# Attention of an AdaLN block: the maxima of two PSUM banks in one VectorE instruction, and the softmax sums dealt out anew between VectorE and GpSimd

## What is computed

```python
pattern = jnp.einsum('bhid,bhjd->bhij', k, q) * scale      # 2048 keys i by 2048 queries j, for 2 x 16 heads
prob = jax.nn.softmax(pattern, axis=-2)                     # over the keys
out = jnp.einsum('bhis,bhid->bhsd', prob, v)
x = x + ga * (concat(out) @ Wo + bo)
```

## Time and profile before

| | us |
|---|---|
| median of 3 runs (4717.35 to 4722.87) | 4717.73 |
| the profiled execution, its own time | 4722.76 |
| its span, first to last instruction | 4721.0 |
| mean granted TensorE clock | 0.972 of full |

### The profile page before, as it was taken

One profiled execution on the slowest core, in us unless ns is written; L12 is line 12 of the kernel. 1 busy time (PEld: TensorE's weight loads), 2 busy tenths in 40 slices (PEclk: granted clock), 3 DMA queues, 4 the chain that ended last, 5 costly groups with the idle time before them and its releaser, 6 DMA issues.

```text
span 4721.0 us, 67306 instructions
## 1 busy us (share of the span) xinstructions
PE 4368.3 (93%) x25496; PEld 2574.1 (55%) x25496; DVE 3253.8 (69%) x4370; ACT 2169.1 (46%) x3523; POOL 2907.6 (62%) x1269
## 2 busy tenths in 40 slices
PE   7999999999999999999999999759998896989898
PEld 5545454454454454554545544337676675767575
DVE  6777877878777877778777787455654545665455
ACT  5444444444444444444444444326565434556442
POOL 2867767667667677677676676526665334666332
PEclk8999999999999999999999999879999998999899
DMA  2000000000000000000000000100000000000001
GB/s 78 6 11 14 7 11 7 14 11 5 15 11 5 11 15 6 11 13 8 11 6 15 11 5 7 40 18 1 1 1 5 33 1 19 1 1 1 1 1 36
DMA packets 81402, 55.74 MB, mean 12 GB/s; under 512 B 48532, under 2 KB 71016, under 8 KB 81128
## 3 DMA queue, kind: packets, MB, share of 16 engines
q1 hardware_dynamic: 81128, 51.92, 4.1%
HBM read 30.66 MB, written 4.19 MB: 7 GB/s over the span
## 4 chain that ended last, share of the span: by engine, by line
POOL 53%; issue 21%; PE 12%; DVE 8%; ACT 4%; POOLq 1%; DMA 0%; DVEq 0%; SPq 0%; ACTq 0%
POOL accp L770 41%; POOL lp L792 4%; PE psum L1665 4%; POOL accp L766 3%; PE psum L1794 2%; POOL rnorm L782 2%; POOL qk_u L787 2%; PE psum L1807 2%; DVE ssq L1262 1%; ACT lp L974 1%; PE psum L1711 1%; ACT qk_sq L958 1%; DVE qk_w L1274 1%; POOL ug_l L820 1%; DVE lneg L1288 1%
## 5 line engine op out<-in xcount | busy, mean ns | idle before, releaser
L770 POOL TENSOR_TENSOR accp<-accp,prob 128x1024 f32<-128x1024 f32 x704 | 1766.9, 2510 | 492.5 <-ACT prob L928 414.0
L928 ACT ACTIVATE prob<-psum 128x1024 f32<-128x1024 f32 x1024 | 1020.0, 1024 | 1461.4 <-PE psum L1518 1383.6
L1159 DVE TENSOR_REDUCE mx<-psum 128x1 f32<-128x512 f32 x1984 | 1276.2, 684 | 347.2 <-PE psum L1485 298.0
L1530 PE MATMUL psum<-prob,vv 128*64 128x512 f32 x4096 | 993.2, 606 | 0.0
L1485 PE MATMUL psum<-kh,qh 64*128 64x512 f32 x2048 | 493.6, 471 | 56.1 <-DVE mx L1159 48.7
L1530 PEld LDWEIGHTS psum<-prob,vv 128*64 128x64 f32 x4096 | 248.7, 136 | 490.3 <-issue 427.3
L1485 PEld LDWEIGHTS psum<-kh,qh 64*128 64x128 f32 x2048 | 205.3, 185 | 522.6 <-DVE mx L1159 442.0
L792 POOL TENSOR_TENSOR lp<-lp,lrcp 128x1024 f32<-128x1024 f32 x128 | 297.9, 2327 | 238.0 <-DVE lrcp L1294 238.0
L1518 PE MATMUL psum<-nm,one 64*128 64x512 f32 x2048 | 428.7, 408 | 13.9 <-ACT prob L928 6.5
L1518 PE MATMUL psum<-qh,kh 64*128 64x512 f32 x2048 | 412.2, 391 | 0.0
L1518 PE MATMUL psum<-qh,kl 64*128 64x512 f32 x2048 | 412.1, 391 | 0.0
(11 more groups left out here) (197 smaller groups left out, 6942.3 us busy)
## 6 DMA issues: line engine op xcount, KB each, us to landing
kl<-kl SPq DMA_DIRECT2D x64, 256.0 KB, 3.8
wqk<-L_attn_Wq SPq DMA_DIRECT2D x64, 64.0 KB, 2.0
rot_l<-const_rot SPq DMA_DIRECT2D x2, 2048.0 KB, 9.3
out<-lpT SPq DMA_DIRECT2D x32, 128.0 KB, 1.7
wqkv_l<-L_ffn_wqkv SPq DMA_DIRECT2D x4, 768.0 KB, 10.7
w_l<-L_ffn_w SPq DMA_DIRECT2D x4, 618.0 KB
wqk<-L_attn_Wk SPq DMA_DIRECT2D x32, 64.0 KB, 2.0
wv_p<-L_attn_Wv SPq DMA_DIRECT2D x16, 128.0 KB, 2.2
```

The source lines that it names most:

```text
L770: pool.tensor_tensor(acc_p[cp][:], first[:], prob[kt % PRING][:], ALU.add).then_inc(pool_sum, 1)
L928: act.activation(prob[t % PRING][:], psum[:, S_BANK + 2 * (t % 2):S_BANK + 2 * (t % 2) + 2, :].rearrange("p a b -> p (a b)"), ACT.Exp, sca ...
L1159: dve.tensor_reduce(mx4[:, e, qt, c:c + 1], ps, AX_X, ALU.max).then_inc(ring_free, 1)
L1530: mm = pe.matmul(psum[j * DH:(j + 1) * DH, O_BANK, :], vv[:, kt, s * DH:(s + 1) * DH], prob[t % PRING][:, j * T:(j + 1) * T], start=(kt == ...
```

## The change

The first two tiles of a VectorE sum are added in one instruction, straight into `acc_d`, in place of a copy and an addition, so a half costs VectorE two instructions and not three (`DVE_OPS`). VectorE's tiles become 8, 10, 12 in half 0 and 1, 3, 10 in half 1. The first addition stands at the values of the second tile. Its first tile stays unread until then, and the exponential that reuses its slot waits for that (`dve_used`). The weights of groups 11 and 12 become 2 and 3. A couple whose two places are neighbouring banks is reduced by one instruction, which frees both places when it ends.

```diff
--- before.py
+++ after.py
@@ -36,13 +36,13 @@
 CP = CHUNKS // 2
 STEPS = CP * KT
 PRING = 4
-SUM_DVE = (3, 7, 11)
-SUM_POOL = tuple(k for k in range(KT) if k not in SUM_DVE)
+SUM_DVE = ((8, 10, 12), (1, 3, 10))
+SUM_POOL = tuple(tuple(k for k in range(KT) if k not in tiles) for tiles in SUM_DVE)
 
 JOIN = -1
-POOL_SEQ = SUM_POOL[1:-1] + (JOIN,) + SUM_POOL[-1:]
-POOL_OPS = len(POOL_SEQ)
-DVE_OPS = len(SUM_DVE)
+POOL_SEQ = tuple(tiles[1:-1] + (JOIN,) + tiles[-1:] for tiles in SUM_POOL)
+POOL_OPS = len(POOL_SEQ[0])
+DVE_OPS = len(SUM_DVE[0]) - 1
 QK_ITEMS, V_ITEMS = CHUNKS, 4
 V_TILES = KT // V_ITEMS
 WO_ITEMS = CHUNKS * HALVES
@@ -307,7 +307,7 @@
 
             weight = [4] * (GROUPS - 1) + [0]
             weight[0] = 1
-            weight[SUM0_GROUP + 1:SUM0_GROUP + 3] = [0, 2]
+            weight[SUM0_GROUP + 1:SUM0_GROUP + 3] = [2, 3]
             for g in outs:
                 weight[g] = 3
             return [-(-COUPLES * sum(weight[:g + 1]) // sum(weight)) for g in range(GROUPS)]
@@ -406,9 +406,13 @@
 
         OFF_S, OFF_POOL, OFF_DVE, OFF_RING = STEPS, CP * POOL_OPS, CP * DVE_OPS, RING_PAIR
 
-        def pool_used(kt):
-
-            return 1 if kt == SUM_POOL[0] else POOL_SEQ.index(kt) + 1
+        def pool_used(cp, kt):
+
+            return 1 if kt == SUM_POOL[cp][0] else POOL_SEQ[cp].index(kt) + 1
+
+        def dve_used(cp, kt):
+
+            return max(SUM_DVE[cp].index(kt), 1)
 
         def phase_end(eng, phase):
 
@@ -758,7 +762,7 @@
             def head_sums(G):
 
                 for cp in range(CP):
-                    for i, kt in enumerate(POOL_SEQ):
+                    for i, kt in enumerate(POOL_SEQ[cp]):
                         n = G * (CP * POOL_OPS) + OFF_POOL + cp * POOL_OPS + i
                         pool.wait_ge(pool_sum, n)
                         if kt == JOIN:
@@ -766,7 +770,7 @@
                             pool.tensor_tensor(acc_p[cp][:], acc_p[cp][:], acc_d[cp][:], ALU.add).then_inc(pool_sum, 1)
                             continue
                         pool.wait_ge(exp_done, G * STEPS + cp * KT + kt + 1)
-                        first = acc_p[cp] if i else prob[SUM_POOL[0] % PRING]
+                        first = acc_p[cp] if i else prob[SUM_POOL[cp][0] % PRING]
                         pool.tensor_tensor(acc_p[cp][:], first[:], prob[kt % PRING][:], ALU.add).then_inc(pool_sum, 1)
 
             with pool.Fori(0, ALL_PAIRS) as p:
@@ -921,10 +925,10 @@
 
                     act.wait_ge(pv_done, G * STEPS + OFF_S + t - PRING + 1)
                     cp, kt = divmod(t - PRING, KT)
-                    if kt in SUM_DVE:
-                        act.wait_ge(dve_sum, G * (CP * DVE_OPS) + OFF_DVE + cp * DVE_OPS + SUM_DVE.index(kt) + 1)
+                    if kt in SUM_DVE[cp % CP]:
+                        act.wait_ge(dve_sum, G * (CP * DVE_OPS) + OFF_DVE + cp * DVE_OPS + dve_used(cp % CP, kt))
                     else:
-                        act.wait_ge(pool_sum, G * (CP * POOL_OPS) + OFF_POOL + cp * POOL_OPS + pool_used(kt))
+                        act.wait_ge(pool_sum, G * (CP * POOL_OPS) + OFF_POOL + cp * POOL_OPS + pool_used(cp % CP, kt))
                     act.activation(prob[t % PRING][:], psum[:, S_BANK + 2 * (t % 2):S_BANK + 2 * (t % 2) + 2, :].rearrange("p a b -> p (a b)"),
                                    ACT.Exp, scale=float(ATT_SCALE)).then_inc(exp_done, 1)
                     if t == KT + 1:
@@ -1154,6 +1158,11 @@
 
             def max_couple(rb, r, k):
                 qt, c = divmod(k, CHUNKS)
+                if (r + 1) % RING:
+                    ring_wait(rb, r + 1)
+                    bank = M_BANK + r % RING
+                    dve.tensor_reduce(mx4[:, :, qt, c], psum[:, bank:bank + 2, :], AX_X, ALU.max).then_inc(ring_free, 2)
+                    return
                 for e in range(2):
                     ps = ring_wait(rb, r + e)
                     dve.tensor_reduce(mx4[:, e, qt, c:c + 1], ps, AX_X, ALU.max).then_inc(ring_free, 1)
@@ -1175,13 +1184,13 @@
                 op.then_inc(ring_free, count)
 
             def add_sum(G, cp, j):
-                kt = SUM_DVE[j]
-                dve.wait_ge(exp_done, G * STEPS + cp * KT + kt + 1)
-                if j:
-                    dve.wait_ge(dve_sum, G * (CP * DVE_OPS) + OFF_DVE + cp * DVE_OPS + j)
-                    dve.tensor_tensor(acc_d[cp][:], acc_d[cp][:], prob[kt % PRING][:], ALU.add).then_inc(dve_sum, 1)
-                else:
-                    dve.tensor_copy(acc_d[cp][:], prob[kt % PRING][:]).then_inc(dve_sum, 1)
+                tiles = SUM_DVE[cp]
+                dve.wait_ge(exp_done, G * STEPS + cp * KT + tiles[j] + 1)
+                left = prob[tiles[0] % PRING]
+                if j > 1:
+                    dve.wait_ge(dve_sum, G * (CP * DVE_OPS) + OFF_DVE + cp * DVE_OPS + j - 1)
+                    left = acc_d[cp]
+                dve.tensor_tensor(acc_d[cp][:], left[:], prob[tiles[j] % PRING][:], ALU.add).then_inc(dve_sum, 1)
 
             def normalise(G, rb, i, hh, cp):
                 ps = ring_wait(rb, i)
@@ -1217,8 +1226,8 @@
                             next_hidden(rb, r, j, places(kind, j, hh))
                         elif kind == "values":
                             cp, kt = divmod(j, KT)
-                            if kt in SUM_DVE:
-                                add_sum(G, cp, SUM_DVE.index(kt))
+                            if kt in SUM_DVE[cp][1:]:
+                                add_sum(G, cp, SUM_DVE[cp].index(kt))
                         elif kind == "sum":
                             normalise(G, rb, r, hh, j)
                         elif kind == "proj_qk":
```

## The result

The kernel with the change takes 5074.93 us in the median (5070.18 to 5077.93), the one before 4718.75 in the same comparison: ratio 1.0752, 95% interval 1.0734 to 1.0771. It is **slower by 7.5%**, by 356 us, where 238 were forecast; the time lies above the range.

What follows compares the result with a forecast made beforehand. PE, working in order and waiting for banks that VectorE frees, was taken to set the time. 15 even heads at +7.0 us and 16 odd-like at +8.3 add 238 us: 4961 profiled, 4956 median, range 4815 to 5035.

Steps and rivals of the forecast that it cites:

- What bounds the kernel: In the attention, PE works in order and sets the time; a couple's successor waits 1.38 us for its first bank.
- The reduce of two banks: Inside groups, merging frees the first bank 0.55 us later; VectorE saves 65 to 120 us; even-head output groups take 6.88.
- (a): End of group 5: step 12's exponential waits for the addition reading tile 8; PE loses 1.5 us in every head.
- (b): End of group 6: GpSimd blocks the addition of tile 12; group 7's next couple is 2.3 (odd) or 1.6 us (even) late.
- (c): End of group 9: step 21's exponential waits for the read of tile 17, 0.6 us in even heads, 1.15 in odd.
- Behind the middle sum: Group 12's first couple waits for the bank of group 11's new couple, 2.15 us late; group 12 takes 6.51.
- the sum: Over groups 1 to 14, even heads +7.0 us and odd heads +8.3, in all 238 us, giving 4956 us.
- the 4.36 for group 14 of the even heads: The time forecast for this group in even heads, in us, with nothing added for an addition ahead of it.
- TensorE's clock: In the attention's PE timings, taken at the full clock; no loss from a falling clock was forecast.
- Faster: Rival: VectorE's own time holds PE in three-couple groups, so shorter reduces gain; 4570 us at best; chance 0.05.
- More locking: Rival: GpSimd slower on half 0's eight tiles, step 12's late read blocked too; 110 us more, 5066; chance 0.12.
- The 49 us: VectorE's saving from 653 merged reduces at 0.075 us fixed cost each; 4669 us if VectorE's time counted fully.

Runs made afterwards that it cites:

- e1_merge_only: The kernel before with only the merged reduce: a couple on neighbouring banks is reduced by one instruction; 5026.01 us, ratio 1.0627.
- e9_merge_last_only: The kernel before with two banks merged only for a group's last couple when the values follow, not in group 0; 4740.03 us, ratio 1.0044.
- e5_filled_waits: The full change plus extra matmuls in PE's longest waits, in group 7 of odd heads and ahead of group 12; 5036.94 us, ratio 1.0673.
- e3_weights_back: The full change with the weights of groups 11 and 12 back at 0 and 2; 4998.08 us, ratio 1.0578.
- e2_no_merge: The full change without the merged reduce, both banks reduced singly again; 4845.02 us, ratio 1.0257.
- e11_both_best: The kernel before with new-form sums on tiles 10, 11, 14 and 2, 3, 10 and merged last couples ahead of values; 4748.23 us, ratio 1.0064.

## Why the prediction was right, and where it failed

- **What bounds the kernel**: right. PE waits in order; VectorE became 120 us lighter and the kernel 356 us slower.
- **The reduce of two banks**: right in the mechanism and per group (5.65 for the forecast 5.61, 6.26 for 6.16, 6.9 for 6.88 with outputs), and shown by taking it away. What it saves VectorE was too high (40 us for 65 to 120). One place was left out: the couple of group 0 in odd heads is reduced behind the last sum of the head before, so group 1 is 0.6 late. The general form is that of e1_merge_only and e9_merge_last_only: the 0.55 us surface wherever VectorE comes late, not only inside three-couple groups.
- **(a), the late read of tile 8**: right, 6.47 and 6.14 against 6.43 and 5.86. **(b)**, the blocked addition of tile 12: right in both heads (5.92 for 6.00, 8.93 for 8.46, and 8.38 in e5_filled_waits). **(c)** about right (5.10 and 6.60 for 4.93 and 6.76).
- **Behind the middle sum**: the wait was right (6.71 for 6.51 in even heads), and e3_weights_back takes it away.
- **The step that failed** is the sum, in two terms that it put at nothing. The first is the 4.36 for group 14 of the even heads, as if nothing stood ahead of it: the addition of tile 26 came 0.1 us behind one of GpSimd's and the group took 6.5 us, 2.15 more in each of 14 heads, 30 us. No experiment moved this addition alone; e2_no_merge shows that group 14 is back at 4.37 where it comes 0.5 us ahead of GpSimd's next. The second is TensorE's clock, held at full throughout: waits of some 2 us were costed at their length or not at all, while the matmuls behind them ran at half the clock. By e5_filled_waits that is 2.7 us an odd head, an estimate of 41 us for the 15 odd heads with maxima, and 1.6 in group 15 of nine even heads, 15 us. Together 86 of the 117 us missing in the profiled execution (5078 against 4961); the largest of the rest are groups 1 (0.6), 6 and 14 (0.3 each) of the odd heads, 18 us.
- **The rivals**: "Faster" had its condition refuted by e1_merge_only: its three-couple groups with one hand-over went from 5.06 to 5.65. "More locking" had a right part (a blocked addition, 2.15 us) in a place it didn't name, ahead of group 14. The 49 us that the forecast worked out for VectorE's saving from a fixed cost per instruction come near the measured 40, but they were worth nothing to PE. The rows that it set beside that cost do not bear it out, though: 1.16 against 2 x 0.67 us is 0.18 saved and not 0.075, and 1.23 against the 1.29 of a pair is 0.06.

Open is why the clock falls in some heads and not in others with like waits (of the 14 even heads with the wait ahead of group 14, it falls behind it in ten, head 30 among them, whose group 15 is short), and why e1_merge_only scatters by 1%.

## What to carry to other kernels

A buffer ring is a loop of start, work and release; merging two units of work shortens the work but frees the first buffer later, and where the producer comes back sooner than that, it waits for the difference (0.55 us here inside three-couple groups, nothing where the next couple came 2.3 us later). Before moving work on a shared engine, list for each place what stands right behind it on that engine and how much wait the next group hides. Where two engines block each other, a change also shifts who comes first: with the same additions and copies, VectorE's took 124 us longer in e1_merge_only. Every variant with the merge had fewer instructions on VectorE than the same kernel without it, and none was faster (e11_both_best is level, all others slower). A long wait of TensorE costs more than its length when what follows runs at half the clock, so read the granted clock behind each long wait.

## What was not expected of the hardware

Idle of 2.5 us on PE was followed by 6.4 us at a granted clock of 0.51, and with matmuls placed into the idle time it stayed at 1.00 there. Whether VectorE's addition of two SBUF tiles takes 1.42 or 3.37 us hung on arriving 0.5 us ahead of a GpSimd addition or 0.1 behind it.
